# A graph layer on Trainium2: a split first layer, one-byte segment numbers and a rearranged node stage

## What is computed

```python
# per edge: e64 = edge_attr_64, sh = edge_attr_9
wk = relu(e64 @ k_w1 + k_b1) @ k_w2 + k_b2          # 64 -> 64 -> 128
wv = relu(e64 @ v_w1 + v_b1) @ v_w2 + v_b2
k  = wk * sum_s sh[:, s] * (x[src] @ Cqk[:, s, :])  # s = 0..8
v  = wv * sum_s sh[:, s] * (x[src] @ Cv[:, s, :])
alpha = softmax over the edges of a target of (q[dst] . k) per head
out = x @ W_self + segment_sum(alpha * v) @ W_out
x1  = layernorm(x + batchnorm(out) * gamma + beta)
agg = segment_mean(e64)
y   = relu(relu([agg, x1] @ W0 + b0) @ W1 + b1) @ W2 + b2
result = layernorm(x1 + y)
```

## Time and profile before

| | before |
|---|---|
| median of three runs | 4953.81 us |
| profiled execution, and its span | 4955.06 us, 4953.1 us |
| PE, DVE, ACT, POOL busy (share of the span) | 95%, 82%, 66%, 73% |
| last slice of the edge loop at full load | 36 of 40 |
| node stage, from its first instruction to the end | 4821.65 to 4953.1 us |

### The profile page before, as it was taken

The page is one execution under the profiler, slowest core; times in us unless marked ns, Lnnn a source line. Parts: engine busy times, 40 slices in busy tenths (PEclk is TensorE's granted clock), DMA queues, the critical chain, the costliest instruction groups (busy, mean ns, idle before and its releaser), DMA issues. The chain is left out here.

```text
span 4953.1 us, 115236 instructions
## 1 busy us (share of the span) xinstructions
PE 4700.8 (95%) x35582; PEld 4437.3 (90%) x35582; DVE 4062.8 (82%) x5044; ACT 3281.4 (66%) x6495; POOL 3598.5 (73%) x3494
## 2 busy tenths in 40 slices
PE   6999999999999999999999999999999999998256
PEld 6899999999999999999999999999999999997243
DVE  4888888888888888888888888888888888886435
ACT  2566667777666666676776666666767766666127
POOL 3777777777777777777777777777777777773460
PEclk9999999999999999999999999999999999998578
DMA  8899999999999999999999999999999999996320
GB/s 220 184 220 219 217 216 217 217 217 215 218 216 217 215 218 217 215 218 216 218 214 219 216 215 217 217 217 215 218 216 217 214 219 217 215 217 147 92 63 27
DMA packets 679343, 1003.23 MB, mean 203 GB/s; under 512 B 105939, under 2 KB 364053, under 8 KB 679045
## 3 DMA queue, kind: packets, MB, share of 16 engines
q1 hardware_dynamic: 560740, 750.71, 69.1%
q0 software_dynamic: 112960, 242.16, 21.0%
q10 hardware_dynamic: 5600, 9.83, 0.7%
HBM read 823.43 MB, written 178.93 MB: 202 GB/s over the span
## 5 line engine op out<-in xcount | busy, mean ns | idle before, releaser
L830 PE MATMUL psum<-chi,zhi 128*128 128x256 f32 x7840 | 2193.1, 287 | 0.0
L833 PE MATMUL psum<-clo,zhi 128*128 128x256 f32 x7840 | 2116.8, 279 | 0.0
L532 POOL DMA_INDIRECT gx<-in_xg,idxs x1568 | 1693.8, 1080 | 474.7 <-issue 473.3
L537 POOL DMA_INDIRECT gq<-qtab,idxs x1568 | 1592.5, 1016 | 477.9 <-issue 477.6
L832 PE MATMUL psum<-chi,zlo 128*128 128x256 f32 x6272 | 1749.8, 279 | 0.0
L688 DVE TENSOR_TENSOR z<-psum,shb 128x1536 f32<-128x1536 f32 (+1 forms) x784 | 1132.5, 1486 | 428.6 <-PE psum L802 428.6
L830 PEld LDWEIGHTS psum<-chi,zhi 128*128 128x128 f32 x7840 | 1473.8, 188 | 2.0 <-issue 2.0
L833 PEld LDWEIGHTS psum<-clo,zhi 128*128 128x128 f32 x7840 | 1473.2, 188 | 0.0
L832 PEld LDWEIGHTS psum<-chi,zlo 128*128 128x128 f32 x6272 | 1179.5, 188 | 1.9 <-issue 1.9
L611 ACT ACTIVATE ot<-psum 128x400 f32<-128x400 f32 x784 | 399.3, 509 | 941.5 <-PE psum L860 940.1
L582 ACT ACTIVATE zhi<-z 128x1536 fp32r<-128x1536 f32 (+1 forms) x784 | 1007.5, 1285 | 1.6 <-DVE z L688 1.5
(11 more groups left out here) (210 smaller groups left out, 6273.5 us busy)
## 6 DMA issues: line engine op xcount, KB each, us to landing
shb<-in_shT SPq DMA_DIRECT2D x392, 640.0 KB
shb<-in_shT SPq DMA_DIRECT2D x392, 512.0 KB
rows<-ot SPq DMA_DIRECT2D x392, 416.0 KB
e<-in_eT SPq DMA_DIRECT2D x392, 128.0 KB
drow<-rankd SPq DMA_DIRECT2D x392, 128.0 KB
gx<-in_xg,idxs POOLq DMA_INDIRECT x1568
gq<-qtab,idxs POOLq DMA_INDIRECT x1568
qtab<-qs ACTq DMA_DIRECT2D x25, 256.0 KB, 6.0
```

What stands on the lines that cost most here:

```text
L532: nc.gpsimd.indirect_dma_start(out=gx[:, s, k, :], out_offset=None, in_=xg[:, :], in_offset=bass.IndirectOffsetOnAxis(ap=ids[:, k:k + 1], ...
L537: nc.gpsimd.indirect_dma_start(out=gq[:, s, k, :], out_offset=None, in_=qtab[:, :], in_offset=bass.IndirectOffsetOnAxis(ap=ids[:, TC + k:T ...
L830: mm(tpb[:, k, :], zhi[:, s, j, e], chi[:, j, :], start=(j == 0), stop=False)
L833: last = mm(tpb[:, k, :], zhi[:, s, j, e], clo[:, j, :], start=False, stop=(j == ST - 1))
```

## The change

- The first layer becomes two f32r products. The weights are split in two parts, `w1hi` and `w1lo`, each on both halves of the partitions. The features of a chunk are split into a first part in f32r and the rest; both stand above each other in the 128 partitions of `es`, so that one product takes both. ScalarE makes the first parts and VectorE the rests, for two chunks at a time, in even steps.
- SyncE's `features` waits for the rests (`eslo_done`) in place of `h_full`.
- The segment numbers are kept and spread as one byte.
- The copies of `o0` also sum their columns (`osum`), and the sum over all of `o0` becomes a sum of 25 columns.
- The node stage works on all 16 blocks in one pass over eight PSUM banks. The mean is taken out by a product with a centring matrix (`cmat` = identity minus mean) and, for the second norm, by weights and bias that are centred beforehand (`cm2`, `cbias`), so there are six products a block. ScalarE has seven operations a block and VectorE seven.

```diff
-        w1 = eb("w1", [P, 2, P])
+        w1hi = eb("w1hi", [P, P], f32r)
+        w1lo = eb("w1lo", [P, P], f32r)
...
-            drow = ms("drow", [P, 2, CH], bf16)
+            drow = ms("drow", [P, 2, CH], u8)
+            es = ms("es", [P, 2, CH], f32r)
...
 # SyncE, features(c)
-                            sp.wait_ge(h_full, c.value() - 2)
+                            sp.wait_ge(eslo_done, c.value() - 2)
...
 # ScalarE, in step after z_first_part(c, 1), if c.r % 2 == 1, for c + 1; once before the loop for chunk 0
+                    def features_first_part(c):
+                        act.wait_ge(e_in[c.r // 2 % 2], 32 * (c.turn(4) + 1))
+                        if c.old(2):
+                            act.wait_ge(h_full, c.value())
+                        for j, d in ((0, slice(0, D)), (1, slice(D, P))):
+                            f(es[d, j, :], e2[d, c.r // 2 % 2, :], ACT.Copy).then_inc(eshi_done, 1)
...
 # VectorE, in step after z_rest(c), if c.r % 2 == 1, for c + 1; once before the loop for chunk 0
+                    def features_rest(c):
+                        dve.wait_ge(eshi_done, c.value() + 2)
+                        if c.old(2):
+                            dve.wait_ge(h_full, c.value())
+                        for j, d, other in ((0, slice(0, D), slice(D, P)), (1, slice(D, P), slice(0, D))):
+                            v.tensor_tensor(es[other, j, :], e2[d, c.r // 2 % 2, :], es[d, j, :].bitcast(fp32),
+                                            ALU.subtract).then_inc(eslo_done, 1)
...
 # TensorE, hidden(c)
-                        pe.wait_ge(e_in[s], 32 * (c.turn(4) + 1))
+                        pe.wait_ge(eslo_done, c.value() + 1)
...
-                        mm(hbank, w1[:, c.r % 2, :], e2[:, s, :], start=True, stop=True).then_inc(h_full, 1)
+                        mm(hbank, w1hi[:, :], es[:, c.r % 2, :], start=True, stop=False)
+                        mm(hbank, w1lo[:, :], es[:, c.r % 2, :], start=False, stop=True).then_inc(h_full, 1)
...
 # node stage, TensorE
+                        product("cy", cmat, "y", lambda j: xp[:, ncols(j)])     # after st_d 7 and centred_made 4
+                        product("var", mn, "sq", of("sq"))
+                        product("z0", m0x, "x1", of("x1"))
+                        product("z1", m1, "h0", of("sq"))
+                        product("z2", cm2, "h1", of("dd"))
+                        product("var2", mn, "sq2", of("sq"))
 # (block j >= 8 of a product waits for the reader of block j - 8, block j < 8 for the reader of block j + 8 of the product before)
 # node stage, ScalarE
+                        each_block("dd", lambda j: f(W("sq", j), W("dd", j), ACT.Square))
+                        each_block("var", lambda j: f(W("sq", j), bank_of(j), ACT.Ln, bias=epsc[:, 0:1]))
+                        each_block("lg", lambda j: f(W("sq", j), W("sq", j), ACT.Exp, scale=-0.5))
+                        each_block("s0", lambda j: f(W("sq", j), W("dd", j), ACT.Relu))
+                        each_block("dd2", lambda j: f(W("sq", j), W("x1", j), ACT.Square))
+                        each_block("var2", lambda j: f(W("sq", j), bank_of(j), ACT.Ln, bias=epsc[:, 0:1]))
+                        each_block("lg2", lambda j: f(W("sq", j), W("sq", j), ACT.Exp, scale=-0.5))
 # node stage, VectorE
-                        v.tensor_reduce(st[:, 0:1], ov, AX.XY, ALU.add).then_inc(st_d, 1)
+                        v.tensor_reduce(st[:, 0:1], osum[:, :], AX.X, ALU.add).then_inc(st_d, 1)
...
+                        each_block(None, lambda j: v.scalar_tensor_tensor(
+                            out=xp[:, ncols(j)], in0=o0[:, ncols(j)], scalar=st[:, 7:8], in1=xp[:, ncols(j)],
+                            op0=ALU.mult, op1=ALU.add))
+                        dve.wait_ge(st_pe, 3)
+                        v.tensor_copy(cbias[:, :], banks[5][:, 0:2]).then_inc(st_d, 2)
...
+                        each_block("cy", lambda j: v.tensor_scalar(W("dd", j), bank_of(j), cbias[:, 0:1], None, ALU.add))
+                        each_block("rs", lambda j: v.tensor_tensor(W("x1", j), W("dd", j), W("sq", j), ALU.mult))
+                        each_block("z0", lambda j: v.tensor_tensor(W("dd", j), bank_of(j), eh[:, ncols(j)], ALU.add))
+                        each_block("z1", lambda j: v.tensor_scalar(W("dd", j), bank_of(j), mb[:, 1:2], 0.0, ALU.add, ALU.max))
+                        each_block("z2", lambda j: v.scalar_tensor_tensor(
+                            out=W("x1", j), in0=bank_of(j), scalar=cbias[:, 1:2], in1=W("x1", j), op0=ALU.add, op1=ALU.add))
+                        each_block("rs2", lambda j: v.tensor_tensor(W("sq", j), W("x1", j), W("sq", j), ALU.mult))
```

More of the change, by code:

```diff
@@ L9 @@
 i32 = mybir.dt.int32
+u8 = mybir.dt.uint8
 ALU = mybir.AluOpType
@@ L168, in gnn_kernel @@
             ctp = ps("ctp", [P, ST, KV])
+            w1 = ps("w1", [P, P])
             w2 = ps("w2", [P, KV])
@@ L650, in step @@
                             z_first_part(c, 1)
+                        if (c + 1).there() and c.r % 2 == 1:
+                            features_first_part(c + 1)
                         if b.there():
@@ L776, in step @@
                             z_rest(c)
+                        if (c + 1).there() and c.r % 2 == 1:
+                            features_rest(c + 1)
                         if t.there():
@@ L890, in _ @@
                     steps(pe, step)
+        edges.close()
         edges.close()
@@ L1266, in gnn_kernel @@
                 junk = f2("junk", [P, 10 * ROWS_OK], bf16)
-                work = {k: f2(f"{k}_", [P, GN, CN]) for k in ("r", "y", "dd", "sq", "lg", "rs", "x1")}
-                work |= {"y2": work["r"], "h1": work["y"], "h0": work["dd"]}
+                work = {k: f2(f"{k}_", [P, NN, CN]) for k in ("dd", "sq", "x1")}
+                cmat, m2t, cm2 = f2("cmat", [P, P]), f2("m2t", [P, P]), f2("cm2", [P, P])
+                bcol, cbias = f2("bcol", [P, 2]), f2("cbias", [P, 2])
                 W = lambda k, j: work[k][:, j, :]
-                bank_of = lambda j: banks[j][:, 0:CN]
-                def ncols(i, j):
-                    return bass.ds(i * GN * CN + j * CN, CN)
+                bank_of = lambda j: banks[j % 8][:, 0:CN]
+                ncols = lambda j: slice(j * CN, (j + 1) * CN)
+                READS = {"cy": "dd", "var": "lg", "z0": "s0", "z1": "h1", "z2": "dd2", "var2": "lg2"}
                 with nc.Block() as block:
@@ L1278, in _ @@
                     def _(sp):
[L1279 to L1284 removed]
+                        for j in range(NN):
+                            wait_made(sp, "o", j)
+                            sp.dma_start(out[:, ncols(j)], W("sq", j)).then_inc(y_s[j % GN], 16)
                         for j in range(GN):
@@ L1290, in _ @@
                         t = nc.tensor
-                        for k in range(2):
-                            pe.wait_ge(st_d, 1 + 2 * k)
-                            t.matmul(banks[k][:, 0:2], fold[:, :], st[:, 2 * k:2 * k + 2], start=True, stop=True).then_inc(st_pe, 1)
-                        def product(name, lhsT, after, src, i):
-                            for j in range(GN):
-                                wait_made(pe, after, i, j)
-                                t.matmul(bank_of(j), lhsT[:, :], W(src, j), start=True, stop=True).then_inc(made_by["pe"], 1)
@@ L1301, in turn @@
-                        def turn(i):
-                            product("mean", mn, "y", "y", i)
-                            product("var", mn, "sq", "sq", i)
-                            product("z0", m0x, "x1", "x1", i)
-                            product("z1", m1, "h0", "h0", i)
-                            product("z2", m2, "h1", "h1", i)
-                            product("mean2", mn, "y2", "y2", i)
-                            product("var2", mn, "sq2", "sq", i)
-                        turns_of(pe, NN // GN, turn)
+                        t.transpose(banks[7][:, 0:P], m2[:, :], idn[:, :]).then_inc(centred_made, 1)
@@ new lines, in _, with product @@
+                        pe.wait_ge(centre_made, 2)
+                        pe.wait_ge(centre_made, 3)
+                        t.matmul(banks[5][:, 0:2], cmat[:, :], bcol[:, :], start=True, stop=True).then_inc(st_pe, 1)
+                        before = None
+                        def product(name, lhsT, after, src):
+                            nonlocal before
+                            for j in range(NN):
+                                wait_made(pe, after, j)
+                                if j >= 8:
+                                    wait_made(pe, READS[name], j - 8)
+                                elif before:
+                                    wait_made(pe, READS[before], j + 8)
+                                t.matmul(bank_of(j), lhsT[:, :], src(j), start=True, stop=True).then_inc(made_by["pe"], 1)
+                            before = name
@@ L1314, in _ @@
                         f = nc.scalar.activation
```

(21 more changed lines are left out.)

91 lines of the change are left out of this document (36 added, 55 removed).

## The result

The change made the kernel slower: 5138.64 us median (5135.79 to 5141.66, 4 runs) against 4953.69 (4952.58 to 4956.01, 4 runs), a ratio of 1.0373 with a 95% interval of 1.0358 to 1.0389. The forecast was 4815.

A forecast was written before the change was run, and what follows sets the result against it. TensorE was taken to bound the edge loop, with GpSimd and DMA close behind. 4955.06 - 118 (loop) - 5.8 (statistics) - 17.0 (node blocks) + 1 (start) = 4815 us, range 4790 to 4860.

The forecast's parts named there:

- TensorE's 10.99 us a chunk: Edge loop: TensorE's time per chunk falls from 11.353 to 10.99 us through the first layer's two f32r products.
- Splitting the features: Edge loop: new copies and subtractions add about 0.55 us a chunk on ScalarE, 0.6 on VectorE; priced at nothing.
- GpSimd's best pace under the loop's full load: Edge loop: GpSimd can go no faster than 11.035 us a chunk, read from index copies between 234.3 and 455.0 us.
- the first rival: Edge loop: TensorE stays the bound, longer gathers vanish with the gate; 137 us saved, 4796 us; chance 0.14.
- the gate: Edge loop: the next chunk's gathers wait for the semaphore of VectorE's L703 (wkq_done); taken to stretch a gather to 1.41 us.
- the rule: Skill text: a VectorE instruction with two SBUF inputs contends with a GpSimd instruction reading SBUF; the loser blocks fully.
- the fourth rival: Edge loop: each new subtraction blocks GpSimd for 0.69 us, giving 11.72 us a chunk; slower, 5074 us; chance 0.05.
- The byte: Edge loop: one-byte segment numbers spread 64 KB less a chunk, taking DMA to 11.05 us (to 11.13).
- The loop's 118 us: Edge loop: pace falls from 11.353 to 11.04 us; 381 chunks at 0.31 us save 118 us.
- Start: Before the first chunk: one feature split, small copies, one memset gone; +1 us (0 to +3).
- Node stage: After the edge loop: statistics save 5.8 us and the one-pass blocks 17.0 us (13 to 20).
- my four rivals: Whole kernel: TensorE bound, 4796 (0.14); DMA bound, 4848 (0.15); loop no faster, 4933 (0.06); GpSimd blocked, 5074 (0.05).

The follow-up runs named there:

- after_shift64: The changed kernel with 64 semaphore increments on ScalarE just ahead of its edge loop: 4935.86 us.
- after_rows: The changed kernel, nothing added ahead of ScalarE's loop, with VectorE's long subtraction (zlo from z and zhi) split into three one-row parts: 5153.25 us.
- rows_rest: after_shift64 with VectorE's long subtraction (zlo from z and zhi) split into three one-row parts: 4794.55 us.
- rows_two_bytes: rows_rest with the segment numbers kept in two bytes again instead of one: 4795.37 us.
- before_rows: The kernel before the change with only VectorE's long subtraction split into three one-row parts: 4934.63 us.
- rows_at128: after_rows with 128 instructions ahead of ScalarE's loop: 5141.20 us.

## Why the prediction was wrong

**TensorE's 10.99 us a chunk: right.** Where nothing stops it, it needs 11.02 to 11.03. The two new products (after_shift64, TensorE's timeline):

```profile
2003.79 0.48 PE L850 MATMUL psum<-es,w1hi 128*128 128x512 f32 x1
2004.11 0.39 PE L851 MATMUL psum<-es,w1lo 128*128 128x512 f32 x1
2004.34 0.84 PE L899 MATMUL psum<-rv,seg 128*128 128x200 f32 x4
```

From 2003.79 to the next product at 2004.34 it is 0.55 us, waits for the copy included; the forecast had 0.47 + 0.03, the old product 0.86.

**"Splitting the features ... Both stay under 11.0, so I price them at nothing": the step that failed.** The busy time of the new work was right. In 1000 to 4000 us of after (busy us, mean ns):

```profile
L742 DVE TENSOR_TENSOR es<-e,es 64x512 fp32r<-64x512 f32 x250 | 170.5, 682 | 3.9
...
L611 ACT ACTIVATE es<-e 64x512 fp32r<-64x512 f32 x250 | 157.9, 631 | 3.0
```

What was missing is that instructions have a cost by their place, too. The change adds 14 recorded instructions to ScalarE's turn and 20 ahead of its loop. That moved the loop's end from 11 to 45 in a block, and 46 stops of 6.4 us came. after_rows against rows_rest prices them by themselves: 5153.25 - 4794.55 = 359 us, 7.8 a stop. By the turn shown above this is TensorE's pause (the stop, less what ScalarE had in hand) and then its 1.2 GHz. The cover that I named (0.5 us a chunk on VectorE; ScalarE at 8.5 of 11.0) was cover for busy time, spread over the chunks. Against one stop of 6 us it is worth little.

**"GpSimd's best pace under the loop's full load" 11.035: failed, hidden behind the first.** I took six copies at the start of the loop for the best pace under load. In after_shift64, where GpSimd sets the pace, it runs at 11.38, since its place beside VectorE's operations is another: the hold-ups are 0.97 us a chunk there and 0.70 between those six copies. My sum for the first rival (eight gathers, 10.0 us, and 0.4 for copy and fetch) had it nearly right but for the hold-ups, which I gave to the gate, though in the kernel before GpSimd never waits for VectorE between 1000 and 4000. The gather of 1052.03 in the earlier trace rows took 1.41 us because VectorE ran rv<-rv, both inputs in SBUF, from 1051.95 to 1052.63; it ended 0.81 us after that, as the others do.

```profile
1051.95 0.68 DVE L696 TENSOR_TENSOR rv<-rv 128x512 f32<-128x512 f32 x1
```

The test I made for the rule was L709 against a gather that began when L709 was nearly over. One pair of records can't refute a rule; the table above, from the same trace, bears it out. The hold-ups beside the long subtraction cost 4935.86 - 4794.55 = 141 us once the stops are gone. The mechanism of the fourth rival was right, in an operation that was there before; its place, the new subtractions, was wrong.

**The byte: the term was wrong.** I had DMA at 11.35 us a chunk with two bytes and at 11.05 to 11.13 with one. With two bytes and both causes gone the loop runs at 11.03 (rows_two_bytes, 223 GB/s). So 217 GB/s was no ceiling, and saving 64 KB gave 0.8 us, inside the interval. The term did the sum no harm only because TensorE's stood at the same height.

**The loop's 118 us: too small, once both causes are gone.** From the first to the last group of transposes rows_rest takes 4310.9 us, before 4444.4: -133.5, near the first rival's 137. TensorE alone then sets the pace, at 11.03.

**Start: small, and of the other sign. Node stage: right.** The first transposes come at 77.1 us instead of 78.4 (forecast +1). From the end of the last copy of `o` to the end of the span it is 5136.6 - 5028.5 = 108.1 us, before 4953.1 - 4821.3 = 131.8: -23.7 against the forecast -22.8.

The sum then: 4955 - 133 - 24 - 1 = 4797, against the 4794.55 of rows_rest. The kernel as it is takes 5138.64 - 4794.55 = 344 us more, and that is the two causes together. The chance of 0.94 for faster rested on a list of costs that had two kinds left out, and my four rivals shared that gap.

## What to carry to other kernels

A loop on one engine can stop at its branch for instruction fetches, 6 us a turn here, and whether it does depends on its length and its place: any edit that adds instructions to such an engine, or ahead of its loop, can set it off. Look at the packets of the instruction queues and at the idle time ("issue") before the loop's first instruction, before judging an edit. Keep the turn short: starting from the same place, a turn of 288 instructions had no stops where one of 317 had them (one case each; by the table its end may count and not its length). With the gathers' cause out of the way as well this was worth 352 us.

Where GpSimd issues gathers and is nearly full, count what VectorE runs when each gather starts. Operations with both inputs in SBUF hold it up until they end, so cut long ones into short parts: two starts more a chunk cost VectorE 0.17 us (2763.21 / 3000 x 11.384 = 10.49, 2898.48 / 3000 x 11.028 = 10.65) and gave 0.36 of pace.

An engine that seems to follow another may have nothing in hand. TensorE and GpSimd both stood at 11.35 here. Look whether the follower ever waits for the other: GpSimd didn't between 1000 and 4000, and did once its hold-ups were shorter (before_rows).

## What the runs showed of the hardware

- ScalarE's instruction fetch: a stop of 6.4 us a turn (up to 7.2 in after, 8.8 in rows_at128) with five packets of 8192 bytes a turn, in a loop of 303 or 317 recorded instructions at six of eight places. The other engines had none of it: in after, between 400 and 4500 us, none stands more than 0.4 us behind its branch.
- After a pause of 4.94 us TensorE was granted 1.2 GHz for some 5 us (0.50 from 1551 to 1555), products 0.21 us apart, then 2.4 GHz and 0.12.
- A gather takes 0.94 us and 1.97 to 2.17 beside a subtraction of 1536 columns with both inputs in SBUF. Beside a product of the same size with one input in PSUM it takes 0.94.
- DMA moved 223 GB/s at a busy share of 0.98 where 217 at 0.98 had looked full.
